# Perceiver layer on one core: rotating the wide queries bank by bank, and another order of loads and first operations

## What is computed

```python
x = x + xattn(layernorm(x), ctx_512, ...)      # x: 2 x 256 x 512, ctx: 2 x 4096 x 128, 16 heads
x = x + attn(layernorm(x), ...)                # products over the heads of one token
x = x + ffn(layernorm(x), ...)                 # gated, quantised weights

def xattn(hidden_q, kv_c, Wq, w_kc_q, w_kc_kv, W_qr, W_kr, Wo):
    q_hk  = (hidden_q @ Wq.T).reshape(B, S, H, K)
    q_big = einsum('bshk,hkq->bshq', q_hk, w_kc_q)          # 384 wide: the wide queries
    q_big = q_big * cos_q + rotate_half(q_big) * sin_q      # the rotation
    kv_r  = kv_c * cos_k + rotate_half(kv_c) * sin_k
    q_r   = einsum('bshq,hqr->bhsr', q_big, W_qr)
    k_r   = einsum('bld,hdr->bhlr', kv_r, W_kr)
    attn  = softmax(einsum('bhsr,bhlr->bhsl', q_r, k_r))
    ctx_c = einsum('bhsl,bld->bhsd', attn, kv_r)
    ...
```

## Time and profile before

| | us |
|---|---|
| median of 3 runs | 1104.91 (1104.62 to 1105.61) |
| profiled execution | 1106.48 |
| its span (first to last instruction) | 1104.7 |
| PE busy | 1033.1 (94%) |
| DVE busy | 855.7 (77%) |
| ACT busy | 799.8 (72%) |
| POOL busy | 498.4 (45%) |

### The profile page before, as it was taken

How to read it: one execution, slowest core, us unless ns; L and a number is a source line. 1 busy time by engine, 2 the same in 40 slices (tenths; PEclk the granted TensorE clock), 3 DMA queues, 4 the chain that set the end, 5 groups by cost and what they waited for, 6 DMA issues and landing times.

```text
span 1104.7 us, 24584 instructions
## 1 busy us (share of the span) xinstructions
PE 1033.1 (94%) x9456; PEld 718.9 (65%) x9456; DVE 855.7 (77%) x1177; ACT 799.8 (72%) x1380; POOL 498.4 (45%) x748
## 2 busy tenths in 40 slices
PE   4899998999999999999799999999999899999988
PEld 3444444666666677667577766776777654859877
DVE  3999888989898988888698898888898813454633
ACT  1233338899999999999799998999999932426532
POOL 1985363566767554545345454545455312000000
PEclk9999999999999999999899999999999999999989
DMA  8443365899999999999999899999998952032000
GB/s 342 132 146 114 109 138 111 180 193 204 198 202 207 207 193 199 190 188 195 192 196 193 201 179 195 192 197 194 201 193 192 192 190 105 1 132 89 1 20 20
DMA packets 568917, 180.15 MB, mean 163 GB/s; under 512 B 551520, under 2 KB 557664, under 8 KB 568160
## 3 DMA queue, kind: packets, MB, share of 16 engines
q1 hardware_dynamic: 567184, 173.33, 72.3%
q10 hardware_dynamic: 1616, 5.24, 1.5%
HBM read 39.07 MB, written 1.05 MB: 36 GB/s over the span
## 4 chain that ended last, share of the span: by engine, by line
PE 57%; DMA 13%; DVE 13%; ACT 10%; issue 6%; POOL 0%; SPq 0%; ACTq 0%; POOLq 0%; DVEq 0%
DMA pt_both<-p_both 13%; PE ps_o L1289 6%; PE ps_o L1290 6%; PE ps_o L1293 5%; PE ps_o L1350 5%; ACT prob L673 5%; DVE sized L973 4%; PE ps_s L1270 3%; PE ps_s L1271 3%; PE ps_s L1272 3%; DVE qcos L892 2%; DVE qrot L888 2%; ACT p_both L664 2%; PE ps_t L1270 2%; ACT oscl L690 2%
## 5 line engine op out<-in xcount | busy, mean ns | idle before, releaser
L962 DVE SCALAR_TENSOR_TENSOR p_both<-prob,p_both 128x1024 f16<-128x1024 f32 x256 | 322.3, 1259 | 87.8 <-ACT p_both L664 87.2
L664 ACT ACTIVATE p_both<-prob 128x1024 f16<-128x1024 f32 x256 | 270.6, 1057 | 34.0 <-DMA pt_both<-p_both 11.7
L1289 PE MATMUL ps_o<-kn,pt_both 128*128 128x128 f16 x2048 | 257.1, 219 | 27.9 <-DMA pt_both<-p_both 27.4
L1290 PE MATMUL ps_o<-kn,pt_both 128*128 128x128 f16 x2048 | 257.0, 219 | 0.0
L1289 PEld LDWEIGHTS ps_o<-kn,pt_both 128*128 128x128 f16 x2048 | 200.0, 98 | 71.7 <-DMA pt_both<-p_both 27.0
L973 DVE TENSOR_SCALAR_CACHE_REDUCE sized<-ps_s,against 128x1024 bf16<-128x1024 f32 x170 | 217.0, 1276 | 0.0
L1290 PEld LDWEIGHTS ps_o<-kn,pt_both 128*128 128x128 f16 x2048 | 200.7, 98 | 24.7
L673 ACT ACTIVATE prob<-ps_s,nmax,unscale 128x1024 f32<-128x1024 f32 x170 | 204.4, 1202 | 11.9 <-DVE sized L973 11.8
L538 POOL TENSOR_TENSOR osum<-oscl 128x256 f32<-128x256 f32 x64 | 47.9, 749 | 257.9 <-ACT oscl L690 257.9
L1293 PE MATMUL ps_o<-kn,pt_both 128*128 128x128 f16 x2048 | 156.6, 219 | 0.0
L1270 PE MATMUL ps_s<-kt,q_hi 128*128 128x512 f16 x340 | 129.3, 380 | 3.5 <-ACT prob L673 2.6
(11 more groups left out here) (215 smaller groups left out, 1849.8 us busy)
## 6 DMA issues: line engine op xcount, KB each, us to landing
wgu_raw<-w_gu_dram SPq DMA_DIRECT2D x11, 512.0 KB, 10.0
wq_s<-wq_t_dram SPq DMA_DIRECT2D x16, 256.0 KB, 3.8
wot_s<-wo_t_dram SPq DMA_DIRECT2D x16, 256.0 KB, 2.8
kvr<-ctx_kv_dram ACTq DMA_DIRECT2D x4, 1024.0 KB, 12.4
pt_both<-p_both SPq DMA_TRANSPOSE x256, 3.8
kvr<-w_mix_dram SPq DMA_DIRECT2D x4, 1024.0 KB, 9.2
wkcq_s<-w_kcq_dram SPq DMA_DIRECT2D x16, 192.0 KB, 2.4
wdn_raw<-w_dn_dram SPq DMA_DIRECT2D x1, 2816.0 KB, 8.9
```

The costliest lines, as they stand in the source:

```text
L664: nc.scalar.mul(p_hi(n), prob[:, n % 2, :], PSCALE).then_inc(hi_done, 1)
L962: nc.vector.scalar_tensor_tensor(out=p_lo(n), in0=prob[:, n % 2, :], scalar=PSCALE, in1=p_hi(n), op0=ALU.mult, op1=ALU.subtract).then_inc( ...
L1289: nc.tensor.matmul(o, pt_hi[:, k, :], kn[:, b, p, 0, keys], start=(k == 0), stop=False)
L1290: nc.tensor.matmul(o, pt_hi[:, k, :], kn[:, b, p, 1, keys], start=False, stop=False)
```

## The change

**The rotation.** `q_rope` works bank by bank. The cosine product of a bank is written over the bank itself in PSUM, after the sine product has read it. The sum then reads one operand from PSUM and one from SBUF and writes `qcos`. Of six instructions (one of 1536 columns, two of 512 on all partitions, two of 512 on 64 partitions, one of 1536) ten are made (all of 512 columns). One counter `rope` counts nine steps a head. PE signals each bank of `q_wide` by itself, in the order 1, 0, 2, and before it writes bank 1, 0 or 2 of the next head it waits for the 6th, 7th or 9th step: for the sum of that bank, not for the sine products. `scores(1)` and R(p) wait for the 9th step.

**The start.** x comes as two halves, one started by SP, one by ACT. Statistics begin on each half by itself. ACT copies the mask first and then starts the loads of the context. `wq_low(0)` stands before the normalisation, `value_weights(0)` before the transposes, the four transposes of the first block begin as each tile is normalised, and H(0) waits for each of its four column blocks separately. SP loads the second block of query weights ahead of the tables, and the value weights ahead of the wide weights.

```diff
@@ SP
-            sp.dma_start(x_in1[:, :, :], x_v).then_inc(x_in, 16)
+            sp.dma_start(x_in1[:, 0:2, :], x_v[:, 0:2, :]).then_inc(x_in[0], 16)
             load_wq(0, 0)
+            load_rest(0, 0)
             load_wkcq(0, 0)
-            load_rest(0, 0)
+            load_wq(1, 1)
             sp.dma_start(cosq[:, :, :].rearrange("p c s -> p (c s)"), cos_q).then_inc(tab_in, 16)
             sp.dma_start(sinq[:, :, :].rearrange("p c s -> p (c s)"), sin_q).then_inc(tab_in, 16)
             load_turn(0, 0)
-            load_wq(1, 1)
...
-                sp.wait_ge(b_done, h + 1)
+                sp.wait_ge(b_done, QC * (h + 1))
@@ ACT
-            act.wait_ge(x_in, 16)
+            act.dma_start(x_in1[:, 2:4, :], x_v[:, 2:4, :]).then_inc(x_in[1], 16)
+
+            act.wait_ge(mask_mm, 1)
+            nc.scalar.copy(mask[:, :], ps_o[:, 0, 0:P]).then_inc(mask_ok, 1)
+            act.wait_ge(x_in[0], 16)
+            act.wait_ge(x_in[1], 16)
             for q in range(4):
...
             round_wq(0, 1)
+            for c in range(DC):
+                act.wait_ge(xnT_mm, c + 1)
+                nc.scalar.copy(xnT_hi[:, c, :], ps_s[:, c, :]).then_inc(xnTh_ok, 1)
+            take_d(0)
             round_wq(1, 1)
             take_qhk(0, 0)
             take_qhk(1, 1)
-            take_d(0)
@@ DVE
+            wq_low(0, 0)
             dve.wait_ge(rstd_ok, 1)
...
-                dve.wait_ge(b_done, h + 1)
-                nc.vector.tensor_tensor(o, q, cosq[:, :, :].unsqueeze(2).to_broadcast([P, QC, B, S]), ALU.mult)
...
-                last.then_inc(rope_mul, 1)
-                dve.wait_ge(rope_mul, h + 1)
-                nc.vector.tensor_tensor(qcos[:, h % 3, :, :], qcos[:, h % 3, :, :], qrot[:, h % 2, :, :],
-                                        ALU.add).then_inc(qrope_ok, 1)
+                def by_cosine(c):
+
+                    nc.vector.tensor_tensor(q[:, c], q[:, c], cosq[:, c, :].unsqueeze(1).to_broadcast([P, B, S]),
+                                            ALU.mult).then_inc(rope, 1)
+
+                def add(c):
+
+                    nc.vector.tensor_tensor(o[:, c], q[:, c], r[:, c], ALU.add).then_inc(rope, 1)
+
+                dve.wait_ge(b_done, QC * h + 1)
+                by_sine(1, whole, whole).then_inc(rope, 1)
+                dve.wait_ge(b_done, QC * h + 2)
+                by_sine(0, whole, whole).then_inc(rope, 1)
+                dve.wait_ge(rope, done + 1)
+                by_cosine(1)
+                dve.wait_ge(rope, done + 2)
+                by_cosine(0)
+                dve.wait_ge(b_done, QC * h + 3)
+                by_sine(2, low, high)
+                by_sine(2, high, low).then_inc(rope, 1)
+                dve.wait_ge(rope, done + 3)
+                add(1)
+                dve.wait_ge(rope, done + 4)
+                add(0)
+                dve.wait_ge(rope, done + 5)
+                by_cosine(2)
+                dve.wait_ge(rope, done + 8)
+                add(2)
@@ PE
-                if not first:
-                    pe.wait_ge(rope_mul, h)
-                for c in range(QC):
-                    last = nc.tensor.matmul(ps_s[:, c, :], wkcq_s[:, i, c * P:(c + 1) * P], qhk[:, i, :],
-                                            start=True, stop=True)
-                last.then_inc(b_done, 1)
+                for k, c in enumerate(ROPE_TURNS):
+                    if not first:
+                        pe.wait_ge(rope, ROPE_STEPS * (h - 1) + (6, 7, 9)[k])
+                    nc.tensor.matmul(ps_s[:, c, :], wkcq_s[:, i, c * P:(c + 1) * P], qhk[:, i, :],
+                                     start=True, stop=True).then_inc(b_done, 1)
...
-                pe.wait_ge(qrope_ok, 2 * p + 2)
+                pe.wait_ge(rope, ROPE_STEPS * (2 * p + 2))
...
-                    pe.wait_ge(rope_mul, H)
+                    pe.wait_ge(rope, ROPE_STEPS * H)
```

More of the change, by code:

```diff
@@ L60 @@
 SOON = 12
+ROPE_TURNS = (1, 0, 2)
+ROPE_STEPS = 9
 def build(nc, x, ctx_kv, wq_t, w_kcq, w_qr, w_kr, w_kckv, wo_t, cos_q, sin_q, cos_k, sin_k,
@@ L190, in build @@
         hT_hi, hT_lo = hT[:, 0, :], hT[:, 1, :]
-        x_in = sem("x_in")
+        x_in = [sem(f"x_in{i}") for i in range(2)]
         x_again = sem("x_again")
@@ L220, in build @@
         qabs_ok = sem("qabs_ok")
-        rope_mul = sem("rope_mul")
-        qrope_ok = sem("qrope_ok")
+        rope = sem("rope")
         kmax_ok = sem("kmax_ok")
@@ L580, in _ @@
                 act.dma_start(kvr[:, :, cols], kv_v[:, :, cols]).then_inc(kv_in[q], 16)
[L581 to L587, removed]
             def round_wq(i, k):
@@ L862, in _ @@
         def _(dve):
-            dve.wait_ge(x_in, 16)
             for t in range(NT):
+                dve.wait_ge(x_in[t // 2], 16)
                 nc.vector.bn_stats(stats[:, t, :], x_in1[:, t, :]).then_inc(st_ln, 1)
@@ L870, in _, with wq_low @@
             nc.vector.tensor_scalar(mv[:, :, 1], mv[:, :, 1], EPS, None, ALU.add).then_inc(var_ok, 1)
+            def wq_low(h, i):
+                dve.wait_ge(wqh_ok, h + 1)
+                nc.vector.tensor_tensor(wq_lo[:, i, :, :], wq_s[:, i, :, :], wq_hi[:, i, :, :].bitcast(F32),
+                                        ALU.subtract).then_inc(wq_ok, 1)
+            wq_low(0, 0)
             dve.wait_ge(rstd_ok, 1)
@@ L876, in q_rope @@
             def q_rope(h):
-                dve.wait_ge(b_done, h + 1)
                 q = ps_s[:, 0:QC, :].rearrange("p c (b s) -> p c b s", b=B)
                 o = qcos[:, h % 3, :, :].rearrange("p c (b s) -> p c b s", b=B)
-                nc.vector.tensor_tensor(o, q, cosq[:, :, :].unsqueeze(2).to_broadcast([P, QC, B, S]), ALU.mult)
                 r = qrot[:, h % 2, :, :].rearrange("p c (b s) -> p c b s", b=B)
-                for dst, src, p0, p1 in ((0, 1, slice(0, P), slice(0, P)), (1, 0, slice(0, P), slice(0, P)),
-                                         (2, 2, slice(0, P // 2), slice(P // 2, P)),
-                                         (2, 2, slice(P // 2, P), slice(0, P // 2))):
+                low, high, whole = slice(0, P // 2), slice(P // 2, P), slice(0, P)
@@ L887, in q_rope, with by_sine @@
+                done = ROPE_STEPS * h
+                def by_sine(src, p0, p1):
+                    dst = (1, 0, 2)[src]
                     sn = sinq[p1, dst, :]
-                    last = nc.vector.tensor_tensor(r[p0, dst, :, :], q[p1, src, :, :],
+                    return nc.vector.tensor_tensor(r[p0, dst, :, :], q[p1, src, :, :],
                                                    sn.unsqueeze(1).to_broadcast([sn.shape[0], B, S]), ALU.mult)
-                last.then_inc(rope_mul, 1)
@@ L905, in _ @@
                                         ALU.subtract).then_inc(xnT_ok, 1)
[L907 to L913, removed]
             wq_low(1, 1)
@@ L1145, in _ @@
             nc.tensor.matmul(ps_o[:, 0, 0:P], period, period, start=True, stop=True).then_inc(mask_mm, 1)
[L1146 to L1151, removed]
             def q_head(h, i, first=False):
@@ L1158, in q_head @@
                 for c in range(DC):
+                    if first:
+                        pe.wait_ge(xnT_ok, c + 1)
                     nc.tensor.matmul(ps_t[:, 0, :], wq_hi[:, i, c, :], xnT_hi[:, c, :], start=(c == 0), stop=False)
@@ L1218, in add_up @@
                 nc.tensor.matmul(o, ones[:, :], parts, start=True, stop=True).then_inc(bound_mm, 1)
+            value_weights(0)
+            for c in range(DC):
+                for t in range(NT):
+                    if c == 0:
+                        pe.wait_ge(xn_ok, t + 1)
+                    last = nc.tensor.transpose(ps_s[:, c, t * P:(t + 1) * P], xn[:, t, c * P:(c + 1) * P], ident[:, :])
+                last.then_inc(xnT_mm, 1)
             q_head(0, 0, True)
@@ L1222, in _ @@
             q_head(1, 1)
-            value_weights(0)
             q_wide(1, 1, 1)
```

## The result

| | before | after |
|---|---|---|
| median, us | 1106.05 (1102.64 to 1111.24, 14 runs) | 1101.01 (1092.83 to 1110.12, 14 runs) |
| ratio of after to before | | 0.9951, 95% interval 0.9929 to 0.9974 |
| `scores(1)` starts, in the profile | 168.88 | 164.67 |

Five microseconds, where 14 were forecast, and outside the range. The longest run of after, 1110.12, was a slow one and isn't in the ratio. Executions of one kernel lie up to 5 us from the median before and up to 9 after, far more than the first three runs showed, and the profiled execution of after was one of the long ones (1106.12). So the two spans can't be compared. The start of `scores(1)` can: it moved by 4.2 us, about what the medians moved.

The account below looks back on a forecast made before the run. DVE's head-after-head chain, slowed by POOL, bounds the projection; the attention is PE-bound. W(15) 14.8 us earlier less 0.8 given back makes 14.0: profiled 1106.5 to 1092.5, median 1090.9, range 1086.5 to 1097.

Parts of the forecast that it names:

- the rotation: DVE's work per head: 6.35 us, against 6.0 before without POOL or 7.85 with it.
- W(9) was forecast 13.0 earlier: Heads 2 to 8: seven heads at 8.47 us, bound by POOL's pieces, so W(9) starts at 96.4 instead of 109.43.
- the end: Last rotation: it can start 1.7 after W(15), takes 6.35, and scores(1) follows 8.1 after W(15), before 7.3.
- three pairs on PE's floor: Heads 9 to 15: three pairs at 16.59 us and two `add_up`, 50.4 against 52.2 before; W(15) at 146.8.
- the 0.8 given back: Last rotation: scores(1) waits for its end, 8.1 after W(15) instead of 7.3, taking 0.8 us off the gain.
- the start: First heads: H(0) at 15.7 to 16.1, W(0) at 22.0, rotation 1 done at 37.1, 6.6 us earlier.
- I count no earlier rise: H(0) on PE: takes 5.48 us as before, at the 1.2 GHz pace, with no earlier change to 2.4 GHz.
- the halves of x: Start: both halves share the transfer engines and land together at about the old time; nothing counted, bound 1 us earlier.
- The loads moved at SP have nothing behind them that would come late: SP's loads at the start: tables are needed at 23, wide weights at 22, so no lateness counted.
- Behind it on PE's queue stand H, V and R, and DVE's next `wq_low` needs none of them: W(9) on PE: its new wait for the sums of rotation 8 costs nothing while PE is the slower one.
- The refill takes over as the bound: Rival, weights of head h+2 after POOL's piece: 0.6 us lost once, 2.6 with longer landing; 1093.5; chance 0.08 with late start.
- the range's lower end: Whole kernel: 1086.5, if `wq_low` doesn't hold POOL (2.8) and x lands 1 us earlier.

Follow-up runs that it names:

- e4: Changed kernel's new rotation and its waits, with loads and first operations of the kernel before; scores(1) at 156.94, timed again median 1098.54 us, ratio to before 0.9914.
- e6: e2 plus scores(1) waiting for the 7th step of the last rotation instead of the 9th; median 1090.45 us, ratio to before 0.9836.
- e2: Changed kernel with SP alone reordered: query weights of head h+3 load ahead of SP's wait for POOL and the tables; scores(1) at 152.40 us.
- e7: Changed kernel with four float32 filler matmuls on PE between W(2) and H(3); scores(1) at 157.09 us.
- e8: Changed kernel with three float32 filler matmuls on PE ahead of H(0), making the start later; scores(1) at 157.24 us.
- e5: Changed kernel's new loads and first operations, with `q_rope` of the kernel before; scores(1) at 165.66 us.
- e11: Kernel before with SP's query weights loaded ahead of its wait for POOL and ACT rounding ahead of its copies; scores(1) at 170.85 us.
- e1: Changed kernel with ACT alone reordered: each `round_wq` ahead of `take_d`, `take_qr` and `take_qabs`; scores(1) at 155.71 us.

## Why the prediction was wrong

**Right: the rotation.** 6.35 a head forecast, 6.48 measured; PSUM as output costs nothing to see, the sums don't wait, POOL's pieces are 7.9 to 8.6 apart. W(9) was forecast 13.0 earlier for both halves; the rotation alone (e4) puts it at 97.9, 11.5 earlier. By the rule of the Trainium skill that was weighed there (VectorE: DVE Perf Modes, "The TRN2 errata") each instruction more would have cost 0.125, an estimate from its 120 cycles. The traces show about half of that: two cosine products take 1.20 above, so three take 1.80 by an estimate, and the one wide product before took 1.67 to the next start, 0.13 less for two instructions fewer.

**Right: the end.** `scores(1)` 8.2 behind W(15), three pairs on PE's floor, PE as busy in the attention. Of the 0.8 given back 0.95 is measured (8.23 less 7.28), and e6 shows that 1.28 of such a wait can be had back.

**Wrong by 3.2, to the safe side: the start.** "I count no earlier rise" of the clock, and nothing for the halves of x. The statistics began 0.6 earlier, H(0) at 14.49 (forecast 15.7 to 16.1), and it ran at the fast pace from 15.86. e2, where nothing stalls, bears out the rest of the sum: W(9) at 93.4 is 3.0 ahead of the forecast, W(15) 2.6, `scores(1)` 2.5 ahead of 154.9.

**The step that failed** is that the sum puts the wait for head 3's weights at nothing. It rests on the sentence "The loads moved at SP have nothing behind them that would come late", with "Behind it on PE's queue stand H, V and R, and DVE's next `wq_low` needs none of them". The first looks at the loads that were moved, and not at the one that stayed: head 3's weights, issued behind SP's wait for POOL's first piece, a time that the rest of the change doesn't move (33.49 before, 33.61 after). PE comes 5.0 us earlier than in e4 and waits 4.9 us more (5.52 against 0.60). The second is false through ACT: `wq_low` needs `round_wq`, which stands behind `take_qr`, which waits for R. That loop is as long as PE's floor and bears no hold.

**The right rival at the wrong size.** "The refill takes over as the bound" named the place. It said 0.6, "once, not per head". By the forecast DVE comes 4.8 after POOL's piece and `wq_low` is possible 5.4 after it. In the trace the piece ends at 32.73, DVE is free at 35.56, 2.8 after it, and `wq_low` starts at 38.80, 6.1 after it: a wait of 3.24, to which POOL adds 1.7 by holding it. And it was worked out as a delay alone. It costs what the clock takes (2.3 by e7) and what the phase takes (5.3) as well. e8 is the case that I had in mind, W(0) at 21.7: there the refill costs 0.81 of wait, W(9) comes at 98.2 and the milestone at 157.2, 2.3 later than forecast, with one hold of 2.75 in it.

In sum, of the 9.8 us that `scores(1)` is later than forecast: 12.3 is what the late load costs against e2, less 2.5 by which all else was better. The 12.3 are 4.9 by which H(3) starts later, 2.5 more by W(3), and 4.9 in the three pairs behind it. A small slip besides: the range's lower end adds up to 1087.1 (1090.9 less 2.8 and 1), not 1086.5.

## What to carry to other kernels

When a change lets one engine arrive earlier, list the things that come at a fixed time whatever it does, here a load behind a wait for another engine, and ask what they do to the earliest arrival. Follow each wait through the queues of all engines until it closes: a loop with no slack against the floor is at the mercy of any hold. And read a change in two halves apart as well as together; here they gave 11.9, 3.2 and 4.2.

## What the runs showed of the hardware

**Idle time and the clock don't go by the length of one gap.** After 5.52 us of idle H(3) ran at 0.43 a matmul. After 2.24 (e5) and 2.41 (e11) it did so for most of its matmuls, then at 0.23; in before H(5) did, at 64.71, after only 1.85. After 3.04 (e1), 2.41 (H(3) in before) and 2.12 (e7, with 3.6 us of work just ahead) it didn't. The same 2.41 stands on both sides. So more counts than the length of the gap; these runs don't say what.

**POOL and DVE keep step.** A DVE instruction with two SBUF inputs that starts 0.07 or 0.09 behind POOL's is held 2.2 us. The next meeting can be like it: two pairs in a row in after, one hold that dissolves in e8. Where it comes just ahead of POOL's, as in e7, POOL is the one held.

**The attention scatters by itself.** From `scores(1)` to the end of the span before took 935.8, after 939.6, e2 937.1, e7 934.1, e6 934.4. The same kernel, with its milestone at 156.94 both times, took 936.8 and 939.8. So single executions don't tell 3 us from nothing here. Part of it can be placed. In those two executions PE's waits for the transposing transfer (`pt_both`) from 170 to 890 us add up to 26.0 and 29.2, the longest of them, near 540 us, being 5.4 and 6.7; in e7 it is 22.7 in all, 3.7 the longest. It isn't the whole: before has 27.4 and after 27.9, with 3.8 us between them. Long executions also have the lower mean granted clock, of after's 1106.12 and 1105.17 at 0.986, 1092.83 at 0.994; which of the two makes the other isn't shown. The milestone, ahead of all that, repeated exactly here, though W(0) of the two executions is 24.1 and 23.9 and W(3) differs by 0.06.
